# Part of the edge comparisons moved from the value projection to the key feature stage, and joined weight banks laid into other waits, six of 32 behind the experts

## The reference, cut to what matters

```python
xn = layernorm(x)
x = x + gcn(xn, edges) + mix0(xn)     # mix0: V, K, Q projections, feature maps, K'V, Q'(K'V), Wo
x = x + experts0(layernorm(x))        # top 2 of 8, capacity 391
xn = layernorm(x)
x = x + sage(xn, edges) + mix1(xn)    # q' = relu((xn @ Wq.T + bq) . P)
x = x + experts1(layernorm(x))
```

## Time and profile before

| what | value |
|---|---|
| median of 3 runs | 3187.97 us (3185.45 to 3194.71) |
| profiled execution, own time | 3187.38 us |
| its span | 3185.4 us |
| mean granted TensorE clock | 0.969 |
| busy, share of the span | PE 94%, PE weight load 87%, VectorE 62%, ScalarE 40%, GpSimd 15% |
| chain that ended last | PE 86%, VectorE 7%, issue 2%, DMA 2% |

### The profile page before, as it was taken

One profiled execution on the slowest core, in us unless ns is written; L12 is line 12 of the kernel. 1 busy time (PEld: TensorE's weight loads), 2 busy tenths in 40 slices (PEclk: granted clock), 3 DMA queues, 4 the chain that ended last, 5 costly groups with the idle time before them and its releaser, 6 DMA issues.

```text
span 3185.4 us, 53094 instructions
## 1 busy us (share of the span) xinstructions
PE 3002.7 (94%) x22248; PEld 2765.1 (87%) x22248; DVE 1983.2 (62%) x3497; ACT 1270.0 (40%) x2176; POOL 462.9 (15%) x328
## 2 busy tenths in 40 slices
PE   8899999999999889999979999999999999979997
PEld 7898898379987778889879999899999999968997
DVE  6986477977876733544456666676355653655665
ACT  3354045444431233433335444544134531424554
POOL 1034443444000111110100000000000000002222
PEclk9999999999999989999989999999999999988999
DMA  7322112123034755755551101363322333248997
GB/s 250 131 59 44 1 16 59 1 51 74 15 86 151 244 142 157 202 154 141 146 148 61 44 27 44 113 153 89 95 78 71 91 90 98 72 137 239 272 281 212
DMA packets 280544, 361.71 MB, mean 114 GB/s; under 512 B 41283, under 2 KB 239465, under 8 KB 278614
## 3 DMA queue, kind: packets, MB, share of 16 engines
q1 hardware_dynamic: 188137, 228.87, 23.6%
q0 software_dynamic: 43312, 77.14, 12.0%
q10 hardware_dynamic: 48829, 51.86, 5.7%
HBM read 273.01 MB, written 84.79 MB: 112 GB/s over the span
## 4 chain that ended last, share of the span: by engine, by line
PE 86%; DVE 7%; issue 2%; DMA 2%; ACT 1%; ACTq 1%; SPq 0%; POOL 0%; DVEq 0%; POOLq 0%
PE PV L515 18%; PE PV L516 18%; PE PV L517 18%; PE PV L685 5%; PE PS L515 3%; PE PS L517 3%; PE PS L516 3%; PE PV L1009 3%; DVE b L2237 2%; PE PA L724 1%; PE PV L915 1%; PE PV L955 1%; PE PA L930 1%; PE PS L930 1%; PE PS L524 1%
## 5 line engine op out<-in xcount | busy, mean ns | idle before, releaser
L515 PE MATMUL PV<-WH,b_split 128*125 128x256 f32 (+2 forms) x4028 | 1174.5, 292 | 41.6 <-DVE b_split L1924 37.1
L516 PE MATMUL PV<-WH,b_split 128*125 128x256 f32 (+2 forms) x4028 | 1159.4, 288 | 2.4 <-issue 2.4
L517 PE MATMUL PV<-WH,b_split 128*125 128x256 f32 (+2 forms) x4028 | 1158.3, 288 | 2.6 <-issue 2.6
L1924 DVE TENSOR_TENSOR b_split<-b,b_split 128x500 fp32r<-128x500 f32 x1008 | 668.7, 677 | 444.5 <-ACT b_split L1504 435.9
L1504 ACT CAST b_split<-b 128x500 fp32r<-128x500 f32 x1008 | 608.4, 613 | 740.9 <-PE PV L517 697.0
L515 PEld LDWEIGHTS PV<-WH,b_split 128*125 128x125 f32 (+2 forms) x4028 | 754.0, 187 | 63.7 <-issue 32.8
L516 PEld LDWEIGHTS PV<-WH,b_split 128*125 128x125 f32 (+2 forms) x4028 | 757.0, 188 | 12.5 <-issue 2.6
L517 PEld LDWEIGHTS PV<-WH,b_split 128*125 128x125 f32 (+2 forms) x4028 | 754.1, 187 | 14.2 <-issue 3.0
L1913 DVE TENSOR_TENSOR WH<-WS,WH 128x1024 fp32r<-128x1024 f32 x292 | 344.4, 1221 | 125.5 <-ACT WH L1494 124.3
L1494 ACT CAST WH<-WS 128x1024 fp32r<-128x1024 f32 x292 | 291.5, 1049 | 182.6 <-PE PV L685 141.1
L1399 POOL DMA_INDIRECT at_d<-ecnt,eidx x168 | 273.9, 1630 | 391.9 <-DMA at_d<-ecnt,eidx 366.7
(11 more groups left out here) (295 smaller groups left out, 3570.3 us busy)
## 6 DMA issues: line engine op xcount, KB each, us to landing
WS<-in_L_ffn_w SPq DMA_DIRECT2D x46, 1024.0 KB, 7.7
WH<-at_d SPq DMA_DIRECT2D x15, 1093.8 KB
WS<-in_L_ffn_gate_w SPq DMA_DIRECT2D x16, 1024.0 KB, 6.6
WS<-in_L_ffn_up_w SPq DMA_DIRECT2D x16, 1024.0 KB, 6.5
WS<-in_L_ffn_down_w SPq DMA_DIRECT2D x16, 1024.0 KB, 5.1
b<-key_d POOLq DMA_DIRECT2D x4, 2560.0 KB, 8.9
WS<-in_L_mix_Wv SPq DMA_DIRECT2D x8, 1024.0 KB, 7.8
WS<-in_L_mix_Wo SPq DMA_DIRECT2D x8, 1024.0 KB, 7.1
```

Of the source, the lines that this page charges most:

```text
L515: pe.matmul(o, a[0], b[0], start=start, stop=False, **kw)
L516: pe.matmul(o, a[0], b[1], start=False, stop=False, **kw)
L517: return pe.matmul(o, a[1], b[0], start=False, stop=stop, **kw)
L1924: ve.tensor_tensor(lo, src, hi.bitcast(F32), ALU.subtract).then_inc(xl_done, 1)
```

## The change

**Edges.** `NOW` = 80 groups are compared in `v0`, in 20 batches from piece 19 on. The other 88 keep their keys in the unused part of the index tile (`late_keys`) and are compared in the key feature stage, one batch behind every third evacuation, 22 batches (`late_edges`). Their rows come in chunks of eight groups (512 KB) on ScalarE's queue, two buffers, each issued at the top of a turn of the head loop (`late_load`). Counts and places are computed in two parts (`places_of`), the second behind evacuation 66. GpSimd waits for the second part before group 80; ScalarE waits for it before it copies head 12, where the scratch lies.

**Joined banks.** None stands ahead of the gates' transposes; half banks 0 to 2 stand between these, 3 to 16 in the ranking, 17 to 23 behind it, 24 and 25 between the two products of `row_tokens`, and 26 to 31 (`ROUTED` = 26) behind the experts. Waits for all 32 become waits for 26. The stage has three places instead of four. The HBM layout of the joined banks is one block of 128 x 1024 per block, so that a store has runs of 4 KB, and a weight unit comes back in two DMAs of one block each in runs of 512 B (`linear_joined`). ScalarE splits the second expert unit before the first half bank instead of before the seventh. The natural query blocks 5 to 7 are loaded behind the last expert's weights, and blocks 13 to 15 stored behind the second value unit of the second layer.

```diff
-JRING = 4
+JRING = 3
+NOW = 2 * EQC
+LATER = 8
+ROUTED = 2 * 13
-            return max(0, j - 24) * (GROUPS // 4) // 40
+            return max(0, j - 17) * (NOW // 4) // 47
...
-            pe.wait_ge(sm_in, 1)
-            for n in range(6):
-                joined(n)
             pe.wait_ge(gates_ready, 1)
...
-                joined(6 + a)
+                joined(a)
...
-                for m in range(9 + 13 * n // 20, 9 + 13 * (n + 1) // 20):
+                for m in range(3 + 14 * n // 20, 3 + 14 * (n + 1) // 20):
...
-            for n in range(22, 28):
+            for n in range(17, 24):
                 joined(n)
-            row_tokens(0, lambda: joined(28))
-            for n in range(29, JOINED):
-                joined(n)
-            pe.wait_ge(jw_copied, JOINED)
+            row_tokens(0, lambda: [joined(n) for n in range(24, ROUTED)])
+            pe.wait_ge(jw_copied, ROUTED)
             experts(0)
+            for n in range(ROUTED, JOINED):
+                joined(n)
             joined_biases()
...
-                    sp.dma_start(pw_d[j // KD][:, pr * P:(pr + 1) * P].rearrange("(k p) c -> p k c", p=P),
-                                 joined_stage(j).rearrange("p (k c) -> p k c", c=P)).then_inc(jw_st[j % JRING], 16)
+                    sp.dma_start(pw_d[j // KD][j % KD], joined_stage(j)).then_inc(jw_st[j % JRING], 16)
...
+            def late_load(c):
+                if c >= 2:
+                    act.wait_ge(eq_used, (NOW + (c - 1) * LATER) // 4)
+                at = (NOW + c * LATER) * P
+                act.dma_start(late_rows(c), key_d.rearrange("g c -> (g c)")[at:at + LATER * P].partition_broadcast(P))\
+                   .then_inc(late_in[c % 2], 16)
...
             for h in range(NH):
+                while n_late < (GROUPS - NOW) // LATER and 6 * (n_late - 1) < 5 * (h + 1):
+                    late_load(n_late)
+                    n_late += 1
+                if h == 12:
+                    act.wait_ge(eidx_ready, 4)
...
                 emptied(ve.tensor_scalar(RB[0:R, n % 4, :], v.read(ve)[0:R, :], 0.0, 0.1, ALU.max, ALU.add))
+                if n % 3 == 2 and NOW // 4 + n // 3 < GROUPS // 4:
+                    late_edges(NOW // 4 + n // 3)
+                if n == 3 * (GROUPS - NOW) // 4:
+                    d.sync()
+                    ve.wait_ge(eq_used, GROUPS // 4)
+                    places_of(slice(NOW, GROUPS), late_keys, late_first, late_srcc)
```

More of the change, by code:

```diff
@@ L416, in build @@
         ws_full = [sem(f"ws_full{i}") for i in range(2)]
+        ws_half = [sem(f"ws_half{i}") for i in range(2)]
         wc_full = [sem(f"wc_full{i}") for i in range(2)]
@@ L470, in build @@
         staged = []
+        joined_units = []
         xs_end = []
@@ L1189, in store_normed, with natural_query, store_joined, linear_joined @@
                         sp.dma_start(natural(pr), A["L1_mix_Wk"][pr * P:(pr + 1) * P, :]).then_inc(nat_in[pr], 16)
-            def store_joined():
-                for j in range(2 * KD):
+            def natural_query(j):
+                sp.dma_start(natural(j), A["L1_mix_Wq"][j * P:(j + 1) * P, :]).then_inc(nat_in[j], 16)
+            def store_joined(blocks):
+                for j in blocks:
                     sp.wait_ge(jw_copied, 2 * (j + 1))
-                    pr = j % KD
-                    sp.dma_start(pw_d[j // KD][:, pr * P:(pr + 1) * P].rearrange("(k p) c -> p k c", p=P),
-                                 joined_stage(j).rearrange("p (k c) -> p k c", c=P)).then_inc(jw_st[j % JRING], 16)
-                    if j < KD:
-                        sp.dma_start(natural(j), A["L1_mix_Wq"][j * P:(j + 1) * P, :]).then_inc(nat_in[j], 16)
+                    sp.dma_start(pw_d[j // KD][j % KD], joined_stage(j)).then_inc(jw_st[j % JRING], 16)
+                    if j + KD < ROUTED // 2:
+                        natural_query(j)
+            def linear_joined(w, vec=None):
+                for q in range(NQ):
+                    u = units[n_unit[0]]
+                    n_unit[0] += 1
+                    sp.wait_ge(wl_done, 2 * (u.stage - 1))
+                    for a in range(2):
+                        sp.dma_start(WS[:, u.stage % 2, :].rearrange("p (k n) -> p k n", k=KD)[:, :, a * P:(a + 1) * P],
+                                     w[2 * q + a].rearrange("p (k c) -> p k c", c=P))\
+                          .then_inc(ws_half[u.stage % 2] if a == 0 else ws_full[u.stage % 2], 16)
+                    if vec is not None:
+                        bias(vec, q)
             def counts(then=None):
@@ L1490, in next_unit @@
                     act.wait_ge(ws_full[u.stage % 2], 16 * (u.stage // 2 + 1))
+                    if u in joined_units:
+                        act.wait_ge(ws_half[u.stage % 2], 16 * (joined_units.index(u) // 2 + 1))
                     if u.place >= 2:
@@ L2251, in _, with places_of @@
             d.sync()
-            ve.wait_ge(eq_used, GROUPS // 4)
-            d(ve.tensor_scalar(first, ecnt[:, :], LATE, None, ALU.is_lt))
-            d.sync()
-            ve.tensor_tensor(ecnt[:, :], ecnt[:, :], first, ALU.mult).then_inc(eidx_ready, 1)
-            d(ve.scalar_tensor_tensor(out=srcc, in0=keyf, scalar=dumpc[:, 0:1], in1=first,
-                                      op0=ALU.subtract, op1=ALU.mult))
-            d.sync()
-            ve.tensor_scalar(eidx[:, :], srcc, dumpc[:, 0:1], None, ALU.add).then_inc(eidx_ready, 1)
+            ve.wait_ge(eq_used, NOW // 4)
+            def places_of(at, keys, first, srcc):
+                d(ve.tensor_scalar(first, ecnt[:, at], LATE, None, ALU.is_lt))
+                d.sync()
+                ve.tensor_tensor(ecnt[:, at], ecnt[:, at], first, ALU.mult).then_inc(eidx_ready, 1)
+                d(ve.scalar_tensor_tensor(out=srcc, in0=keys, scalar=dumpc[:, 0:1], in1=first,
+                                          op0=ALU.subtract, op1=ALU.mult))
+                d.sync()
+                ve.tensor_scalar(eidx[:, at], srcc, dumpc[:, 0:1], None, ALU.add).then_inc(eidx_ready, 1)
+            places_of(slice(0, NOW), keyf[:, 0:NOW], first[:, 0:NOW], srcc[:, 0:NOW])
             def heads_bias(g):
@@ L2303, in _, with late_edges @@
             head_pieces(0, 3)
+            def late_edges(m):
+                g0 = 4 * m
+                c = (g0 - NOW) // LATER
+                if (g0 - NOW) % LATER == 0:
+                    ve.wait_ge(late_in[c % 2], 16 * (c // 2 + 1))
+                d.sync()
+                ve.wait_ge(eq_used, m)
+                for q in range(4):
+                    g = g0 + q
+                    at = g - NOW - c * LATER
+                    ins = ve.scalar_tensor_tensor(out=late_eqs[:, q, :], in0=late_rows(c)[:, at * P:(at + 1) * P],
+                                                  scalar=late_keys[:, g - NOW:g - NOW + 1], in1=late_mask,
+                                                  op0=ALU.is_equal, op1=ALU.mult, accum_out=ecnt[:, g:g + 1])
+                    if q == 3:
+                        ins.then_inc(eq_used, 1)
+                    else:
+                        d(ins)
+            d(ve.tensor_scalar(late_mask, low[:, :], LATE, 1.0, ALU.mult, ALU.add))
             for n in range(2 * KD * NB):
```

64 lines of the change are left out of this document (43 added, 21 removed).

## The result

| what | value |
|---|---|
| median of 4 runs after | 3143.09 us (3140.87 to 3149.28) |
| median of 4 runs before, same chips | 3186.71 us (3180.07 to 3194.71) |
| ratio, 95% interval | 0.9866 [0.9848, 0.9883]: faster by 1.3% |
| profiled execution, own time / span | 3144.12 / 3142.3 us |
| mean granted TensorE clock | 0.974 |

The account below looks back on a forecast made before the run. TensorE was taken to bound nearly all of the kernel, VectorE the value stage. The terms -24.4 + 1.5 - 2.5 - 4.2 + 2.5 = -27.1 us gave 3161 us by the median, range 3152 to 3172.

Parts of the forecast that it names:

- the value stage: First value projection, where edge groups are compared: fewer batches there let TensorE set the pace, -24.4 us (bounds -25.0 and -19).
- the clumps: Value stage: a weight unit, an evacuation and a batch together delay VectorE by 3.96 us; 0.6 us taken for them.
- the late batches: Key feature stage: 22 batches hidden by TensorE's steps, with +1.5 us for late chunks (bounds 0 and 6).
- The three close chunks: Key feature stage: the first load, 2 and 7 land close to need; 1.0 us for the start, 0.25 for each other.
- Rival (a): Key feature stage: GpSimd's scatters delay the late batches, at most 12 us, 3173, or 5.4 us, 3166; chance 9%.
- before the gates: Gates' transposes no longer stand behind six half banks: -2.5 us, half taken for the low clock (bounds -5.3 and 0).
- rival (b): Ranking behind the gates: the low clock lasts into it, part 2 brings nothing, the time is 3168; chance 6%.
- before the experts: Last rank to expert transposes: last three half banks leave the path, -5.5 + 1.1 + 0.2 = -4.2 us (bounds -5.5 and -2).
- The seventh half bank: Behind the last rank: seven half banks instead of six make token numbers come 1.1 us later.
- between the layers: Gap behind the experts: six half banks fit, but three stores of 512 KB compete for DMA, +2.5 us (bounds 0 and 4.2).

Follow-up runs that it names:

- edges_alone: Only the edge part of the change, joined banks as in the kernel before: 3164.13 us, ratio 0.9925 to the kernel before.
- joined_alone: Only the joined-bank part of the change, edges as in the kernel before: 3169.14 us, ratio 0.9943 to the kernel before.
- all_ahead: The changed kernel with all 32 half banks ahead of the experts, none moved behind them: 3160.28 us, ratio 0.9922 to the kernel before.

## Why the prediction was wrong

**Right: the value stage.** -24.0 against -24.4, and edges_alone gave 22.2 us for the part (forecast 22.9). TensorE's own pace sets the stage; the clumps cost about what was taken for them.

**Priced too high: the late batches.** The stretch grew by 2.8 us for a forecast of 1.5, but that nearness is luck: the 2.8 are not the batches'. edges_alone, which has them, takes 743.0 us there, and joined_alone, which has none, 746.4 (before 743.9, after 746.7). Over all profiled kernels it is 743.0 to 747.1 with late batches (twelve) and 743.9 to 746.9 without (five). The three close chunks, from which the 1.5 was made, cost VectorE 0.23 us in all and TensorE nothing: its one wait at the start of the stage is 0.9 us before as well. About half of the 2.8 arises in the query projection behind (547.62 - 415.32 = 132.3 before, 527.39 - 393.55 = 133.8 after), at a clock of 0.98 instead of 0.99; joined_alone has the same there. What lowered it was not tested. Rival (a) didn't occur: GpSimd's scatters ran on, and a comparison took 0.35 us beside one and without one.

**Mis-sized: before the gates.** -5.3, the lower bound, for -2.5. Half of the gain was given to a low clock that lasted 3 us, mostly over transposes of 125 columns, and was over before the ranking, so that rival (b) didn't occur either.

**Mis-sized: before the experts.** -5.7 for -4.2. The seventh half bank behind the last rank cost 0.9 us, near the 1.1 charged, and the second one in the wait for the weights was hidden as forecast (TensorE waited 1.08 us there before and waits 0.18 now). What was too small is the gain of 5.5 for the three last half banks: from the row products to the first expert transposes are 17.65 us before (1107.13 to 1124.78) and 11.12 after (1082.48 to 1093.60), 6.5 less. The row products themselves ran at a higher clock (0.87 instead of 0.71; 4.07 us instead of 4.97), and GpSimd's second gather no longer waits for a half bank at all.

**Mis-sized: between the layers.** +5.7 for +2.5, above my bound of 4.2. The stores cost 4.0, near that bound. The rest is the table load, which no term held: I counted the waits that the change adds on ScalarE by what they wait for, and not by what the compiler places around them.

**The step that failed.** The five stretches of the terms measured sum to -26.5, and the forecast to -27.1 (nearer than the terms deserve, since the 2.8 is no effect of the change). What is missing is a stage that the sum put at nothing without a reason: it has no term for the experts, whose code the diff doesn't touch. Their stretch became 13.5 us shorter because TensorE's code stood elsewhere, 96 instructions earlier. The runs show it from both sides: 96 idle products give the kernel before the short stretch (14 us), 32 take it from the changed kernel (8.7 us by the medians, 12.3 in the stretch), shifts by 256 or 512 instructions change it by under 2 us, and without branches there are no pauses. Over the sixteen profiled kernels that have the branches the stretch lies at 446 to 451 us or at 458 to 465, never between.

**Open.** The 4.2 us after the second layer's first transposes. Over the kernels with the same second layer this distance lies between 1568.5 and 1578.8 us without order by position or by part; some of it may be position as well, since that layer has branches too. Why positions near 0 are long and those at 128 and 160 short is open, too.

## What to carry to other kernels

Before a gain of 10 us is put down to an edit, move the code without it: add idle instructions at a place where the engine waits, and see whether the distance between two far events changes. With its large branches this kernel has such a term of up to 15 us (464.7 and 449.6 us for all_ahead at two positions), and an edit that moves instructions across them draws a new value of it. Count the instructions in the trace, not in the program: I took 64 idle products for 128 instructions, they were 256, and two runs that confirmed the period looked like misses. A table of distances between the same events in both traces finds it at once; look in it for the stretches that the diff doesn't touch.

Work moved into a gap brings its transfers along: the gap between two layers was idle for TensorE and full for DMA, and three stores cost there what six half banks had cost ahead.

## What the runs showed of the hardware

- Pauses of TensorE by issue of 2.4 to 5.5 us behind branches, with a packet of its instruction queue beside them. They come or go with the position of the code, are the same again after 256 instructions (461.0 and 462.7 us, 447.5 and 446.5 us), and are none without branches.
- A stretch of 5180 instructions without branches took 20 packets of 16.4 KB; with 24 branches 5080 instructions took 39.
- A product of two fp32 operands is two matmuls and two weight loads: 64 of them in the program are x128 and x128 in the trace.
- Behind idle time of TensorE the granted clock is 0.50 for a while, with matmuls of 392 columns 0.33 us apart instead of 0.18. The dozen behind the longest pause is there with shorter waits too, so it can't be booked on the pause; over the stretch the half clock is some 2.5 of the 13.5 us.
- VectorE's comparisons of two operands in SBUF took 0.345 us beside GpSimd's scatters (50 of the 88 late ones) and 0.346 without.
- An accumulating scatter beside 1.5 MB of stores landed 3 us later (6.9 to 10.0 us of waiting).
- A table load of ScalarE (1.28 us) stands behind semaphore waits that are written ahead of its activation: three waits that were already satisfied moved it from an idle stretch onto the path.
